# A graph attention kernel: the edge sort and the dense units beside it are rearranged over four engines

## The chip, the cores and the metric

One core of a Trainium2 chip runs the whole kernel. The metric is the device time of one execution in microseconds (us). Of the kernel before, three executions took 1775.53, 1776.36 and 1778.52 us; their median is 1776.36 us. Engines are named as the profile names them: PE is TensorE's matmul, PEld its weight load, DVE is VectorE, ACT is ScalarE, POOL is GpSimd, SP is SyncE (here it only issues DMAs).

## The reference

Four graph layers and four feed-forward layers follow each other on 384 nodes of 512 features, with 12288 edges. The change touches only the first, L0_gnn:

```python
x1 = x[edges[0]]; x2 = x[edges[1]]                 # 12288 x 512 each
e = jnp.concatenate([x1, x2], axis=1) @ Ww + bw    # Ww is 1024 x 1024, 8 heads of 128
e = e.reshape(-1, H, 2 * HD).transpose(1, 0, 2)
e = jax.nn.leaky_relu(e, 0.01)
w = (e @ Wa + ba)[..., 0]                          # one score for each edge and head
mat = jnp.full((H, n, n), -jnp.inf).at[:, edges[0], edges[1]].set(w)
mat = jnp.nan_to_num(jax.nn.softmax(mat, axis=-1))
y = jnp.matmul(mat, (x @ Wv + bv)...)              # then elu, residual, layer norm
```

Everything behind it (an expert layer, a four-block sparse attention, a second expert layer, two more graph layers, a routed attention layer) is the same program before and after.

## The kernel before, in words

`x[edges] @ Ww` is not computed for each edge. The upper and the lower half of `Ww` are each applied once to the 384 nodes, and the edges then pick rows of the products. These products are made by twelve dense **units**: half r (2) by column half q (2) by node tile t (3), each a 128x512 block. On PE a unit is four f32 matmuls over 128 rows each (`pe_rows`, L420), and for r = 1 a fifth that adds the bias from a single row (L427). Each product is kept as three bf16 pieces: ACT copies the top piece (`top_part`, L1057), DVE subtracts it (L1258), ACT copies the middle piece (L1066), DVE subtracts that (L1252). DVE also multiplies the product by `Wa` (L1261) and sums over each of four heads (L1266): the linear part of leaky_relu. These DVE steps are `split_unit`.

The edges are sorted at the same time. Each of the 12288 edges (96 tiles of 128) has a slot: row `q_f`, place `r_f` in it, and a key that holds both ends, `slo1`. For a tile, two 128x128 matrices are made: `slot_one` (1 where the column is the edge's row) and `spread` (the key where the column is the edge's place). PE multiplies the two and adds over all 96 tiles in one PSUM bank, "sortk". The work goes in twelve **groups** of 8 tiles (UN = 8). In each, POOL makes 7 of the 8 slot_one (L1161, POOLED = 7), DVE the eighth (L1298) and all 8 spread (L1299). Both buffers are double: group g waits until PE has used group g - 2 (`sort_used`).

PE's order is written out by hand: two units, then the groups, with one unit behind each group named in AFTER_GROUP; then two transposes of the sorted keys (L938), the last two units, and the loop. DVE's order likewise: `split_unit` behind the groups named in SPLIT_AFTER, `tile_chunks` (L1278 on) behind group 2; at the end it splits the keys out of the bank (L1309 to L1315), and after that the last three units and the small steps that open the loop.

Behind its 84 slot operations POOL issues 20 indirect DMAs that scatter edge records into `tab_bucketed` (L854, at most two not landed), and only then it makes the one-hot edge matrices of the loop (`hot_edges`, L1173, two operations a tile) from tile 4 on. DVE makes those of tiles 0 to 3. The **loop** handles 104 tiles of sorted slots; in each PE gathers the product rows by 12 matmuls and the edge matrix by one (it waits there for `hote_made`). POOL then also issues one indirect DMA a tile (L1185).

SP's queue holds, in order: x, the weights of the units, six fills of `tab_w`, two small fills, and then waits for the keys; behind the keys it fills `tab_x` with twelve DMAs (L1691). After the loop PE makes `x @ Wv + bv` in three more units with a bias row each (`l0o0` to `l0o2`, L1012), beside DVE's row maxima and ACT's exponentials (L1091).

## Time and profile before

| | |
|---|---|
| median of 3 executions | 1776.36 us (1775.53 to 1778.52) |
| the profiled execution's own time | 1784.84 us |
| its span | 1783.1 us, 23533 instructions |
| mean granted clock of PE | 0.967 of full speed |
| PE busy | 1662.2 us (93%), 7303 matmul records |
| DVE busy | 883.9 us (50%) |
| POOL busy | 652.3 us (37%) |
| ACT busy | 500.9 us (28%) |

The profile is of one execution. Its times count from the span's start. An engine's busy share is a mean over stages that have different limits; the part that the change touches lies between 18 and 110 us, and a small one at 408 to 423 us. An f32 matmul of one instruction is two records in the trace. Where a row joins several instructions ("x7"), its second number runs from the start of the first to the end of the last; consecutive operations of an engine overlap slightly, so the time from start to start is a little under the duration.

### The profile page before, as it was taken

Reading aid. Unit: us, or ns where it says so; the run is one execution under the profiler, and the core shown is the slowest. Engines: PE = TensorE matmul, PEld = TensorE weight load, DVE = VectorE, ACT = ScalarE, POOL = GpSimd, SP = SyncE. Lnnn points to the kernel's source line nnn. Section 1 sums busy time; section 2 is a strip of 40 time slices with the busy share of each in tenths; the row PEclk is TensorE's granted clock in tenths of the full one; section 3 lists DMA queues with packets and bytes.
Section 4 is the critical chain, followed back from the end, with each engine's and each line's share of the span. In section 5 each row is a group of like instructions: output and inputs, shape, how many; then the busy total and the mean of one; then the engine's idle time right before and its main releaser. Section 6 shows DMA issues by size and latency. Waiting matters only on the chain.

```text
span 1783.1 us, 23533 instructions
## 1 busy us (share of the span) xinstructions
PE 1662.2 (93%) x7303; PEld 940.2 (53%) x7304; DVE 883.9 (50%) x2161; ACT 500.9 (28%) x1586; POOL 652.3 (37%) x756
## 2 busy tenths in 40 slices
PE   6989999999899999999999998797899999999998
PEld 4534444446655546455556766432444555555655
DVE  8878888888834443443443157785623101111322
ACT  1134444447422414133231225110200111111234
POOL 5868787873232323324342613666200000000000
PEclk9999999999999999999998997899899999999999
DMA  8031101005423123232216734356326121310020
GB/s 315 1 104 25 60 25 60 25 8 132 141 58 128 54 90 83 58 110 55 74 49 153 276 96 146 111 162 174 100 72 217 50 91 53 100 59 24 5 68 18
DMA packets 119614, 161.76 MB, mean 91 GB/s; under 512 B 49497, under 2 KB 61721, under 8 KB 119154
## 3 DMA queue, kind: packets, MB, share of 16 engines
q1 hardware_dynamic: 93056, 115.43, 21.0%
q0 software_dynamic: 18592, 29.91, 6.3%
q10 hardware_dynamic: 7890, 15.44, 2.7%
q8 instruction: 44, 0.72, 0.2%
q14 instruction: 32, 0.26, 0.1%
HBM read 145.26 MB, written 15.47 MB: 90 GB/s over the span
## 4 chain that ended last, share of the span: by engine, by line
PE 81%; DVE 9%; DMA 5%; issue 2%; ACT 2%; POOL 1%; ACTq 0%; DVEq 0%; POOLq 0%; SPq 0%
PE psum L373 79%; DMA ring<-tab_h,sd_t 2%; DMA arena<-tab_h,sd_t 1%; DVE stats L470 1%; DVE ring L1299 1%; DVE xn L2067 0%; PE psum L1028 0%; DVE xn L2073 0%; POOL ring L630 0%; DVE xn L2086 0%; ACT xT L414 0%; PE psum L2302 0%; DMA x<-in_x 0%; DVE ring L666 0%; DMA tab_h<-arena 0%
## 5 line engine op out<-in xcount | busy, mean ns | idle before, releaser
L373 PE MATMUL psum<-arena 128*128 128x384 f32 (+9 forms) x1804 | 315.3, 331 | 21.1 <-DVE arena L2688 8.0
L373 PE MATMUL psum<-arena,ring 128*128 (+1 forms) x1504 | 326.0, 363 | 9.5 <-issue 6.2
L373 PE MATMUL psum<-xT,ring 128*128 128x384 f32 x928 | 310.7, 495 | 6.8 <-ACT xT L414 4.2
L373 PE MATMUL psum<-ring,arena 128*128 128x512 f32 (+1 forms) x570 | 262.8, 604 | 15.3 <-DVE ring L666 10.5
L373 PEld LDWEIGHTS psum<-arena 128*128 128x128 f32 (+5 forms) x1804 | 195.1, 154 | 148.8 <-issue 74.7
L373 PE MATMUL psum<-ring,xT 128*128 128x512 f32 x552 | 251.1, 608 | 1.1 <-issue 0.7
L373 PEld LDWEIGHTS psum<-xT,ring 128*128 128x128 f32 x928 | 178.2, 193 | 133.2 <-issue 17.6
L373 PEld LDWEIGHTS psum<-arena,ring 128*128 128x128 bf16 (+1 forms) x1504 | 139.4, 115 | 131.3 <-issue 29.9
L373 PEld LDWEIGHTS psum<-ring,arena 128*128 128x128 f32 (+1 forms) x570 | 99.2, 187 | 140.4 <-issue 139.3
L1079 ACT ACTIVATE ring<-ring 128x128 f32<-128x128 f32 x416 | 123.3, 297 | 173.4 <-DVE ring L1365 161.4
L373 PEld LDWEIGHTS psum<-ring,xT 128*128 128x128 f32 x552 | 104.8, 195 | 124.1 <-issue 121.7
L854 POOL DMA_INDIRECT tab_bucketed<-rec,pos x96 | 95.6, 996 | 196.8 <-DMA tab_bucketed<-rec,pos 189.3
L2159 POOL DMA_INDIRECT tab_sorted<-rec,pos x104 | 100.2, 963 | 167.0 <-DMA tab_sorted<-rec,pos 143.6
L1365 DVE SCALAR_TENSOR_TENSOR ring<-psum,wa 128x1024 f32<-128x1024 f32 x104 | 127.3, 1224 | 60.8 <-PE psum L373 60.5
L1173 POOL TENSOR_SCALAR arena<-iota,arena 128x128 bf16<-128x128 f32 x200 | 121.9, 617 | 16.3 <-DVE xT L1379 13.5
L1185 POOL DMA_INDIRECT tab_w<-xT,pair x104 | 109.5, 1053 | 46.7 <-DMA tab_w<-xT,pair 29.5
L414 ACT ACTIVATE arena<-psum 128x384 f32<-128x384 f32 (+1 forms) x130 | 61.9, 498 | 180.4 <-PE psum L373 155.6
L373 PE MATMUL psum<-zeros 128*128 128x256 f32 (+3 forms) x383 | 92.3, 398 | 8.6 <-issue 2.9
L373 PEld LDWEIGHTS psum<-zeros 128*128 128x128 f32 (+1 forms) x383 | 71.0, 212 | 23.7 <-issue 9.3
L488 ACT ACTIVATE std<-mv,eps_col 128x1 f32<-128x1 f32 x57 | 16.8, 294 | 224.8 <-DVE mv L471 218.8
L630 POOL DMA_INDIRECT ring<-tab_h,sd_t x61 | 65.2, 1069 | 36.2 <-DMA ring<-tab_h,sd_t 16.0
L1079 ACT ACTIVATION_READ_ACCUMULATOR ring<-ring 128x1 f32 x416 | 77.6, 186 | 0.0
(478 smaller groups left out, 1737.0 us busy)
## 6 DMA issues: line engine op xcount, KB each, us to landing
ring<-in_L_ffn_w SPq DMA_DIRECT2D x22, 1024.0 KB, 7.3
ring<-in_L_gnn_m_w SPq DMA_DIRECT2D x8, 1024.0 KB, 6.1
ring<-in_L_ffn_expert_weights SPq DMA_DIRECT2D x8, 1024.0 KB, 5.5
ring<-tab_key ACTq DMA_DIRECT2D x24, 256.0 KB
ring<-in_L_gnn_Wv SPq DMA_DIRECT2D x5, 1024.0 KB, 5.0
tab_w<-xn SPq DMA_DIRECT2D x6, 768.0 KB, 15.3
ring<-in_L_gnn_Ww SPq DMA_DIRECT2D x4, 1024.0 KB, 18.6
ring<-in_L_gnn_wq SPq DMA_DIRECT2D x4, 1024.0 KB, 5.3
```

The lines of the kernel that those rows point to most:

```text
L373: return nc.tensor.matmul(o, a, b, start=start, stop=stop)
L414: nc.scalar.activation(dst, b[:, 0:w], ACT.Copy).then_inc(banks.free_of(name), 1)
L470: od.link(nc.vector.bn_stats(stats[:, t, :], src[:, t, :]))
L488: nc.scalar.activation(std[:, t:t + 1], mv[:, t, 1:2], ACT.Sqrt, bias=eps_col[:, 0:1]).then_inc(row_std, 1)
L630: return nc.gpsimd.indirect_dma_start(o, None, table, bass.IndirectOffsetOnAxis(ap=column.bitcast(U32), axis=0), **more)
L854: nc.gpsimd.indirect_dma_start(tab_bucketed, bass.IndirectOffsetOnAxis(ap=pos[:, q:q + 1].bitcast(U32), axis=0), rec[:, q, :], None).then_ ...
L1079: last = nc.scalar.activation(prod2[:, b % 2, h, :], prod2[:, b % 2, h, :], ACT.Copy, accum_out=w_sum[:, b, h:h + 1])
L1173: last = nc.gpsimd.tensor_scalar(edge_is[:, j, k, s_, :], iota[:, 0:P], key_rq[:, s_, T:T + 1], None, ALU.is_equal)
L1185: nc.gpsimd.indirect_dma_start(tab_w, bass.IndirectOffsetOnAxis(ap=pair[:, q:q + 1].bitcast(U32), axis=0), w_edge0[:, q, :], None).then_in ...
L1299: last = V.tensor_scalar(spread[:, g % 2, j, :], iota[:, 0:P], r_f[:, t:t + 1], slo1[:, t:t + 1], ALU.is_equal, ALU.mult)
L1365: V.scalar_tensor_tensor(out=prod2[:, b % 2], in0=z_bank[:, b % 2], scalar=0.0, in1=wa_all, op0=ALU.max, op1=ALU.mult).then_inc(z_free, 1)
L2159: nc.gpsimd.indirect_dma_start(tab_sorted, bass.IndirectOffsetOnAxis(ap=pos2[:, q:q + 1].bitcast(U32), axis=0), rec[:, q, :], None).then_i ...
```

## The change

- **Keys in the slot rows.** `slot_key` holds the key where `slot_one` held a 1, made by an operation with two steps (compare, then multiply by the key), and POOL makes 6 of 8 instead of 7 (L1191 of the new kernel), DVE 2 (L1334).
- **Places by one operation.** The 8 spread matrices of a group become one DVE tensor_tensor over 128x1024 (`place`, L1336): the iota row repeated over the tiles against `r_f` repeated over the columns. DVE's operations of a group go from 9 of 128 columns to 2 of 128 and 1 of 1024.
- **Bias.** The biases bw and bv are packed over 128 partitions, split by POOL into three bf16 pieces (four small operations ahead of the slots), stored and loaded again by two DMAs on SP, and added by a bf16 matmul of three rows in place of an f32 matmul of one row: in six units and in `l0o0` to `l0o2`.
- **Head sums by ACT.** For the first nine units four ACT activations with an accumulated sum take the place of DVE's reduction, and DVE waits for them before it writes the product buffer two units later.
- **Order.** PE does four units ahead of the first group, and the other six of the middle behind groups 1, 2, 4, 5, 7 and 9; none stands behind group 11. `slo1` is completed earlier on DVE, as POOL now reads it.

POOL's order before, from the last fill of constants to the loop:

```order
L780 MEMSET arena 128x400
L1161 TENSOR_SCALAR ring<-iota,xT 128x128 x84
L854 DMA tab_bucketed<-rec,pos 13312x4 x20
L1173 TENSOR_SCALAR arena<-iota,arena 128x128 x6
L1185 DMA tab_w<-xT,pair 160768x8
```

The same place in the changed kernel:

```order
L788 MEMSET arena 128x400
L791 CAST bias_parts<-packed 128x12
L792 TENSOR_TENSOR bias_left<-packed,bias_parts 128x12
L793 CAST bias_parts<-bias_left 128x12
L794 TENSOR_TENSOR bias_parts<-bias_left,bias_parts 128x12
L1191 TENSOR_SCALAR ring<-iota,xT 128x128 x72
L869 DMA tab_bucketed<-rec,pos 13312x4 x20
L1204 TENSOR_SCALAR arena<-iota,arena 128x128 x6
L1216 DMA tab_w<-xT,pair 160768x8
```

The slot operations go from 84 to 72, four small ones stand ahead of them, and what follows keeps its order. PE's order before, from the bucket matmul to the second unit with a bias (`ring,xT` x4 is a unit, `ring` x8 a group, `rows,ones` a bias):

```order
L373 MATMUL psum<-gate,ones_b 128x9
L373 MATMUL psum<-ring,xT 128x512 x8
L373 MATMUL psum<-ring 128x128 x16
L373 MATMUL psum<-ring,xT 128x512 x4
L373 MATMUL psum<-ring 128x128 x8
L373 MATMUL psum<-ring,xT 128x512 x4
L373 MATMUL psum<-ring 128x128 x16
L373 MATMUL psum<-ring,xT 128x512 x4
L373 MATMUL psum<-ring 128x128 x8
```

The same place in the changed kernel:

```order
L381 MATMUL psum<-gate,ones_b 128x9
L381 MATMUL psum<-ring,xT 128x512 x16
L381 MATMUL psum<-ring 128x128 x16
L381 MATMUL psum<-ring,xT 128x512 x4
L381 MATMUL psum<-ring 128x128 x8
L381 MATMUL psum<-ring,xT 128x512 x4
L381 MATMUL psum<-ring 128x128 x16
L381 MATMUL psum<-ring,xT 128x512 x4
L381 MATMUL psum<-bias_b,ones_b 128x512
```

Four units (x16 matmuls) now stand ahead of the first two groups, where two did, and the unit behind a given group has a number higher by two, so the first one with a bias comes two units sooner.

```diff
--- before.py
+++ after.py
@@ -227,7 +227,10 @@
 
-        rows = sb("rows", [1, 1552])
+        rows = sb("rows", [1, 16])
+        bias_left = sb("bias_left", [P, 12])
+        bias_parts = sb("bias_parts", [P, 3, 12], BF16)
+        bias_b = sb("bias_b", [3, 3 * D], BF16)
         bc = sb("bc", [P, 7, D])
...
@@ -424,7 +432,7 @@
             if bias is not None:
-                last = mm(b[:, 0:n], ones[0:1, :], bias, False, True)
+                last = mm(b[:, 0:n], ones_b[0:3, :], bias, False, True)
             last.then_inc(banks.full_of(name), 1)
...
@@ -778,6 +786,12 @@
             nc.gpsimd.memset(no_edge, -1.0).then_inc(clear_ready, 1)
+            pool.wait_ge(params, PARAMS)
+            bias = pk("L0_gnn_biases")
+            op.link(nc.gpsimd.tensor_copy(bias_parts[:, 0, :], bias))
+            op.link(nc.gpsimd.tensor_tensor(bias_left[:], bias, bias_parts[:, 0, :], ALU.subtract))
+            op.link(nc.gpsimd.tensor_copy(bias_parts[:, 1, :], bias_left[:]))
+            nc.gpsimd.tensor_tensor(bias_parts[:, 2, :], bias_left[:], bias_parts[:, 1, :], ALU.subtract).then_inc(bias_split, 1)
 
...
@@ -841,11 +855,12 @@
         UNITS = [(r, q, t) for r in range(2) for q in range(2) for t in range(NT)]
-        EARLY = 2
-        AFTER_GROUP = {1: 2, 2: 3, 4: 4, 5: 5, 7: 6, 8: 7, 10: 8, 11: 9}
+        EARLY = 4
+        AFTER_GROUP = {1: 4, 2: 5, 4: 6, 5: 7, 7: 8, 9: 9}
         SPLIT_AFTER = {0: 0, 1: 1, 3: 2, 4: 3, 6: 4, 7: 5, 9: 6, 10: 7, 11: 8}
         KEY_BASE = 256.0
-        POOLED = UN - 1
+        BY_ACT = 9
+        POOLED = UN - 2
         AHEAD = 20
...
@@ -879,6 +894,10 @@
             sp.dma_start(tab_sorted[0:EW * P].rearrange("(p a) k -> p (a k)", p=P), no_edge).then_inc(sorted_cleared, 16)
+            sp.wait_ge(bias_split, 1)
+            sp.dma_start(tab_bias.rearrange("k (p j) -> p k j", p=P), bias_parts[:]).then_inc(bias_stored, 16)
+            sp.wait_ge(bias_stored, 16)
+            sp.dma_start(bias_b[:], tab_bias).then_inc(bias_in, 16)
             banks.drained(sp, "sortk")
...
@@ -908,24 +927,25 @@
             mm(b[:, 16:16 + NBK], ones_b[:], total_b, True, True).then_inc(banks.full_of("bucket"), 1)
-            pe.wait_ge(params, PARAMS)
 
                 r, q, t = UNITS[u]
+                if r == 1 and q == t == 0:
+                    pe.wait_ge(bias_in, 16)
                 if t == 0:
 
-            unit(0)
-            unit(1)
+            for u in range(EARLY):
+                unit(u)
             sort_bank = banks.at
                 pe.wait_ge(slot_hot, g + 1)
-                pe.wait_ge(spread_made, g + 1)
+                pe.wait_ge(place_made, g + 1)
                 for j in range(UN):
                     t = UN * g + j
-                    last = mm(sk[:, 0:P], slot_one[:, g % 2, j, :], spread[:, g % 2, j, :], t == 0, t == ET - 1)
+                    last = mm(sk[:, 0:P], slot_key[:, g % 2, j, :], place[:, g % 2, j, :], t == 0, t == ET - 1)
                 last.then_inc(sort_used if g < ET // UN - 1 else banks.full_of("sortk"), 1)
...
@@ -1058,12 +1078,22 @@
 
+            def heads_of(u):
+                r, q, t = UNITS[u]
+                banks.drained(act, unit_name(u))
+                for h in range(4):
+                    last = nc.scalar.activation(prod_l[:, u % 2, h, :], prod_l[:, u % 2, h, :], ACT.Copy,
+                                                accum_out=lin0[:, r, t, 4 * q + h:4 * q + h + 1])
+                last.then_inc(lin_summed, 1)
+
             top_part(0)
                 nc.scalar.activation(unit_part(u, 1), left_f[:, u % 2, :], ACT.Copy).then_inc(bf16_made, 1)
+                if u < BY_ACT:
+                    heads_of(u)
             act.wait_ge(sorted_cleared, 16)
...
@@ -1158,7 +1188,8 @@
                     t = UN * g + j
-                    last = nc.gpsimd.tensor_scalar(slot_one[:, g % 2, j, :], iota[:, 0:P], q_f[:, t:t + 1], None, ALU.is_equal)
+                    last = nc.gpsimd.tensor_scalar(slot_key[:, g % 2, j, :], iota[:, 0:P], q_f[:, t:t + 1], slo1[:, t:t + 1],
+                                                   ALU.is_equal, ALU.mult)
                 last.then_inc(slot_hot, 1)
...
@@ -1222,6 +1253,7 @@
             V.tensor_copy(total_b, before9[:, :, ET - 1]).then_inc(bucket_ready, 1)
+            V.scalar_tensor_tensor(out=slo1, in0=dlo1, scalar=KEY_BASE, in1=slo1, op0=ALU.mult, op1=ALU.add)
 
...
@@ -1255,13 +1286,19 @@
                 b = banks.filled(dve, unit_name(u))
+                if u >= 1:
+                    banks.drained(dve, unit_name(u - 1))
                 V.tensor_tensor(left_f[:, u % 2, :], b, unit_part(u, 0), ALU.subtract).then_inc(pieces_made, 1)
                     low_part(u - 1)
+                if u >= 2:
+                    dve.wait_ge(lin_summed, min(u - 1, BY_ACT))
                 V.tensor_tensor(prod_l[:, u % 2], b.rearrange("p (h d) -> p h d", h=4), wa_bc,
                     low_part(u).then_inc(parts_made, 1)
+                if u < BY_ACT:
+                    return None
                 banks.drained(dve, unit_name(u))
...
@@ -1292,13 +1329,13 @@
                     dve.wait_ge(sort_used, g - 1)
-                for j in range(UN):
+                for j in range(POOLED, UN):
                     t = UN * g + j
-                    if j >= POOLED:
-                        V.tensor_scalar(slot_one[:, g % 2, j, :], iota[:, 0:P], q_f[:, t:t + 1], None, ALU.is_equal)
-                    last = V.tensor_scalar(spread[:, g % 2, j, :], iota[:, 0:P], r_f[:, t:t + 1], slo1[:, t:t + 1],
-                                           ALU.is_equal, ALU.mult)
-                last.then_inc(spread_made, 1)
+                    V.tensor_scalar(slot_key[:, g % 2, j, :], iota[:, 0:P], q_f[:, t:t + 1], slo1[:, t:t + 1],
+                                    ALU.is_equal, ALU.mult)
+                V.tensor_tensor(place[:, g % 2], iota[:, 0:P].unsqueeze(1).broadcast_to([P, UN, P]),
+                                r_f[:, UN * g:UN * g + UN].unsqueeze(2).broadcast_to([P, UN, P]),
+                                ALU.is_equal).then_inc(place_made, 1)
                 if g == 2:
...
@@ -1335,6 +1372,7 @@
             od.link(split_unit(len(UNITS) - 1, True))
+            dve.wait_ge(lin_summed, BY_ACT)
             V.tensor_scalar(lin0[:, 0], lin0[:, 0], 0.01, None, ALU.mult)
```

## Rows read from the trace of the kernel before

**Rows 1.** Busy time by stretch: PE, PEld, DVE, ACT, POOL; then clock, DMA share, GB/s.

```profile
25.00:50.00 25.00, 17.85 (x83) 12.92 (x83) 24.59 (x71) 3.57 (x6) 25.00 (x39) 0.86 0.52 212
50.00:75.00 25.00, 25.00 (x116) 15.18 (x114) 24.46 (x70) 3.35 (x6) 23.93 (x39) 1.00 0.01 2
```

**Rows 2.** The chain of waits in order of time: start, us, what (two pieces).

```profile
49.70 40.16 PE psum L373 x184
...
105.08 24.59 PE psum L373 x136
```

**Rows 3.** Groups of instructions, 20 to 200 us: busy, mean ns, idle before and releasers.

```profile
L1161 POOL TENSOR_SCALAR ring<-iota,xT 128x128 f32<-128x128 f32 x84 | 53.9, 660 | 22.6 <-DVE xT L1240 19.6 <-PE psum L373 3.0
...
L1079 ACT ACTIVATE ring<-ring 128x128 f32<-128x128 f32 x125 | 37.1, 297 | 58.8 <-DVE ring L1365 55.8 <-issue 3.0
...
L854 POOL DMA_INDIRECT tab_bucketed<-rec,pos x20 | 19.9, 993 | 15.0 <-DMA tab_bucketed<-rec,pos 10.5 <-issue 4.5
...
L1266 DVE TENSOR_REDUCE mask_dst<-ring 128x4 f32<-128x512 f32 x12 | 8.2, 685 | 0.4
```

**Rows 4.** PE in order of time: start, us, engine, line, operation, count.

```profile
64.02 3.60 PE L373 MATMUL psum<-ring,xT 128*128 128x512 f32 x8
67.55 1.12 PE L373 MATMUL psum<-rows,ones 1*128 1x512 f32 x2
68.60 2.05 PE L373 MATMUL psum<-ring 128*128 128x128 f32 x16
...
83.32 2.05 PE L373 MATMUL psum<-ring 128*128 128x128 f32 x16
```

**Rows 5.** POOL in order of time, slots, first record DMA, first hot edges.

```profile
24.49 32.02 POOL L1161 TENSOR_SCALAR ring<-iota,xT 128x128 f32<-128x128 f32 x49 [19.62 <-DVE xT L1240]
...
77.22 4.17 POOL L1161 TENSOR_SCALAR ring<-iota,xT 128x128 f32<-128x128 f32 x7 [1.89 <-PE psum L373]
81.57 1.21 POOL L854 DMA_INDIRECT tab_bucketed<-rec,pos  x1 [0.19 <-issue]
...
116.26 3.51 POOL L1173 TENSOR_SCALAR arena<-iota,arena 128x128 bf16<-128x128 f32 x6
```

**Rows 6.** One line in 37.8 to 37.9 us: ns min/median/max of two operations.

```profile
L1161 POOL TENSOR_SCALAR ring<-iota,xT x2: 594/928/1263, 37.3 to 37.9; 128x128 f32<-128x128 f32 x2
```

**Rows 7.** The same line in 33.3 to 33.4 us.

```profile
L1161 POOL TENSOR_SCALAR ring<-iota,xT x2: 594/774/953, 32.8 to 33.4; 128x128 f32<-128x128 f32 x2
```

**Rows 8.** DVE in order of time at these two places.

```profile
33.18 0.68 DVE L1252 TENSOR_TENSOR arena<-ring,arena 128x512 bf16<-128x512 f32 x1
...
37.65 1.01 DVE L1278 TENSOR_TENSOR cnt_dst<-iota,gate 128x832 f32<-128x832 f32 x1
```

**Rows 9.** POOL in order of time: an operation of two steps, one of one.

```profile
1122.34 1.00 POOL L2616 TENSOR_SCALAR arena<-arena 128x224 f32<-128x224 f32 x1
1123.42 0.77 POOL L2617 TENSOR_SCALAR arena<-arena 128x224 f32<-128x224 f32 x1
```

**Rows 10.** DVE in order of time, behind the key copy.

```profile
90.53 0.69 DVE L1258 TENSOR_TENSOR ring<-psum,arena 128x512 f32<-128x512 f32 x1 [1.81 <-issue]
```

**Rows 11.** PE in order of time: edge matmuls of tiles 0, 1 and 4.

```profile
105.90 0.31 PE L373 MATMUL psum<-arena 128*128 128x128 bf16 x1
...
110.44 0.22 PE L373 MATMUL psum<-arena 128*128 128x128 bf16 x1
...
118.77 0.22 PE L373 MATMUL psum<-arena 128*128 128x128 bf16 x1
...
119.29 1.45 PE L373 MATMUL psum<-arena,ring 128*128 x6
```

**Rows 12.** The loop's first stretch, PE alone: busy, clock, DMA share, GB/s.

```profile
105.00:109.50 4.50, 4.42 (x13) 0.50 0.03 5
```

**Rows 13.** DVE, then ACT, in order of time after the loop.

```profile
423.20 0.17 DVE L1430 TENSOR_SCALAR gate<-gate 128x8 f32<-128x8 f32 x1
...
424.40 1.03 ACT L1091 ACTIVATE arena<-ring,gate 128x384 f32<-128x384 f32 x1
```

More of the change, by code:

```diff
@@ L265, in gnn_ffn_program @@
         slot_hot = sem("slot_hot")
-        spread_made = sem("spread_made")
+        place_made = sem("place_made")
         sort_used = sem("sort_used")
+        lin_summed = sem("lin_summed")
+        bias_split = sem("bias_split")
+        bias_stored = sem("bias_stored")
+        bias_in = sem("bias_in")
         keys_stored = sem("keys_stored")
@@ L348, in gnn_ffn_program @@
         mixT = pk("L2_ffn_mixer_w").rearrange("p (c e) -> p c e", c=KC)
-        r_bw, r_bv0 = rows[0:1, 0:1024], rows[0:1, 1024:1536]
-        r_rb2, r_mixb = rows[0:1, 1536:1539], rows[0:1, 1540:1548]
+        r_bw, r_bv0 = bias_b[:, 0:2 * D], bias_b[:, 2 * D:3 * D]
+        r_rb2, r_mixb = rows[0:1, 0:3], rows[0:1, 4:12]
         BC = {nm: bc[:, j, :] for j, nm in enumerate(WIDE)}
@@ L360, in gnn_ffn_program @@
         tab_key = nc.dram_tensor("tab_key", (P, 2 * P), BF16, kind="Internal").ap()
+        tab_bias = nc.dram_tensor("tab_bias", (3, 3 * D), BF16, kind="Internal").ap()
         tab_w = dram("tab_w", (N * N + ST * P, H8))
@@ L794, in gnn_ffn_program @@
         slot5 = ring.slot(5).rearrange("p c n -> p (c n)")
-        spread = slot6.rearrange("p (b t r) -> p b t r", b=2, t=UN)
-        slot_one = slot7.rearrange("p (b t q) -> p b t q", b=2, t=UN)
+        place = slot6.rearrange("p (b t r) -> p b t r", b=2, t=UN)
+        slot_key = slot7.rearrange("p (b t q) -> p b t q", b=2, t=UN)
         left_f = slot5[:, 0:1024].rearrange("p (b n) -> p b n", b=2)
@@ L1243, in _ @@
             V.scalar_tensor_tensor(out=pos[:], in0=r_f, scalar=float(ST), in1=q_f, op0=ALU.mult, op1=ALU.add).then_inc(pos_ready, 1)
-            od.link(V.scalar_tensor_tensor(out=slo1, in0=dlo1, scalar=KEY_BASE, in1=slo1, op0=ALU.mult, op1=ALU.add))
             dve.wait_ge(params, PARAMS)
@@ L1315, in _ @@
             V.tensor_copy(key_b, key_f).then_inc(banks.free_of("sortk"), 1)
-            od.link(split_unit(len(SPLIT_AFTER)))
+            split_unit(len(SPLIT_AFTER))
             b = banks.filled(dve, "keyT")
@@ L3259 @@
 CHUNKED = dict(L0_ffn_w_gating=6, L1_ffn_w_gating=16, L2_ffn_mixer_w=8)
-TALL = dict(L1_gnn_f_b1=1, spread_f_b2=1, L1_gnn_f_w1=16, spread_f_w2=P, L3_ffn_r_w2=3)
+TALL = dict(L1_gnn_f_b1=1, spread_f_b2=1, L1_gnn_f_w1=16, spread_f_w2=P, L0_gnn_biases=12, L3_ffn_r_w2=3)
 SPREAD = dict(L0_gnn_ba=1, L2_gnn_et_emb=64, L0_gnn_Wa=P)
@@ L3275, in laid_out @@
     inputs["spread_f_w2"], inputs["spread_f_b2"] = w2.reshape(16, P), b2.reshape(P)
+    inputs["L0_gnn_biases"] = _np.concatenate([inputs["L0_gnn_bw"].reshape(-1), inputs["L0_gnn_bv"].reshape(-1)])
     blocks = inputs["L1_gnn_s1_w"].shape[0]
@@ L3298, in laid_out @@
         put(name, _np.broadcast_to(inputs[name].reshape(1, n), (P, n)))
-    rows = _np.zeros((1, 1552), _np.float32)
-    for o, name in ((0, "L0_gnn_bw"), (1024, "L0_gnn_bv"), (1536, "L3_ffn_r_b2"), (1540, "L2_ffn_mixer_b")):
+    rows = _np.zeros((1, 16), _np.float32)
+    for o, name in ((0, "L3_ffn_r_b2"), (4, "L2_ffn_mixer_b")):
         a = inputs[name].reshape(-1)
```

## The prediction

> **What bounds the kernel now.** I read the busy time by stretch first. From 25 to 75 us three engines are full at once: DVE 24.6 and 24.5 of 25 us, POOL 25.0 and 23.9, PE 17.9 and 25.0 [rows 1]. Then the chain of waits: from 49.7 us it runs through PE for 40.2 us [rows 2]. By that alone a change that shortens PE's and DVE's work should pay. But POOL has a line of its own, and I followed it to its end. It begins its slot operations at 24.49 us and ends them at 77.22 + 4.17 = 81.39; 3.0 us of that are waits, 53.9 are busy [rows 3, 5]. Behind them stand 20 record DMAs, and the first one-hot edge operation starts at 116.26, so 34.9 us after the slots [rows 5]. Six of those take 3.51 us, about 0.58 from start to start, so tile 4, the first that POOL serves, is ready at about 117.4. PE used it at 118.77 [rows 11]. POOL's line is thus only 1.3 us from being the one that PE waits for in the loop, and the chain does not show it because it ends just in time. From tile 4 on PE sets the loop's pace, (118.77 - 110.44) / 3 = 2.78 us a tile, so a delay at tile 4 is not made up. The question is therefore when POOL finishes its slots.
>
> **POOL's slots.** There are 72 operations in place of 84, with two steps instead of one.
> - One step, undisturbed: 0.594 us long [rows 6], 0.58 from start to start. The same count before is 84 x 0.58 = 48.7 of the 53.9 busy us, so 5.2 us were blocking by DVE.
> - The second step: two POOL operations of 224 columns took 1.00 with two steps and 0.77 with one [rows 9]. If those 0.23 us go by columns it is 0.13 at 128; if they are fixed it is 0.23; nothing is the lower end. I take 0.13, since one step costs more at 224 columns (0.77) than at 128 (0.594), which says that columns count. So 72 x 0.71 = 51.1 us.
> - Blocking that was there: DVE's tensor_tensor with both inputs in SBUF holds POOL's next operation. At 33.18 us L1252 runs 0.68 us, and the POOL operation that begins in it takes 0.953 instead of 0.594 [rows 7, 8]; at 37.65 L1278 runs 1.01 us, and the next one takes 1.263 [rows 6, 8]. Both held operations, less their undisturbed 0.594, start their work about 0.1 us before DVE's end. The one that was already under way was not stretched. After: eight of L1252's kind at 0.36, one L1278 at 0.67, together 3.6 us.
> - Blocking that is new: `place` is of L1278's kind, both inputs broadcast in SBUF, with 1024 columns instead of 832: 1.01 + 192 x 0.88 / 832 = 1.21 us. It holds POOL for 1.21 - 0.1 less what is left of the operation under way, on the mean half of 0.71: 0.75 us. Twelve of them make 9.0 us. The ends are 0 (hidden in waits) and 1.11 each.
> - Sum: 24.5 + 51.1 + 3.6 + 9.0 = 88.2 us against 81.4, 6.8 us later. That is 5.3 us a group. Waits for `sort_used` fall away at this pace: PE needs 1.9 us for a group (70.49 to the next unit less 68.60) and 3.5 for a unit [rows 4], and has each buffer back before POOL comes to it.
>
> **From the slots to the loop.** The 20 record DMAs keep their 34.9 us: 10.5 of them are waits for landings [rows 3], while SP's twelve fills of `tab_x` go out; those follow the keys and still fall inside. Tile 4 is ready at 88.2 + 34.9 + 1.2 = 124.3. How soon would PE want it? The last group's matmuls ended at 83.32 + 2.05 = 85.4 [rows 4] and now end at 88.2 + 1.9 = 90.1, 4.7 later; behind the key copy the DVE stood idle for 1.81 us on account of unit 9 [rows 10], which now is done before. So the loop opens 2.9 us later, at 108.0 for 105.1 [rows 2], and tile 4 would be wanted at 121.7. POOL is last, PE waits 2.6 us, and tile 4 moves from 118.8 to 124.3: +5.5 us.
>
> **The clock.** Before, PE opened the loop at a granted clock of 0.50, the lower of its two levels (1.2 GHz), after it had waited for DVE [rows 12]; tile 0 to tile 1 took 4.54 us instead of 2.78, so a fall costs 1.8 us [rows 11]. That cost is now hidden under POOL's lateness, but the new wait at tile 4 may bring another. The ends are 0 and 1.8; I take 0.9.
>
> **What does not come through.** The four early units fill PE's wait ahead of group 0, but POOL makes group after group at its own pace, so the time returns as waits behind units. The bias: 1.05 us before (68.60 - 67.55), now a bf16 matmul of 512 columns, six of which take 1.45 us in the loop, 0.24 each [rows 4, 11]; 0.8 saved in six units, all under POOL. The head sums take 0.69 us a unit from DVE [rows 3] and give ACT four times about 0.3 us in a stretch where it is busy 3.6 of 25 us [rows 1, 3]; DVE had become free anyway. If that cover were gone, as with a late ACT, it would cost DVE at most 1.2 us a unit. POOL's four bias operations run in its idle 19.6 us before the slots [rows 3]; the two bias DMAs stand on SP before nothing but the keys, 60 us ahead of them. Behind the loop the three bias rows save PE 2.4 us, but ACT's exponentials then wait for DVE's last maximum, ready at 423.37, where they began at 424.40 [rows 13]: 1.0 us comes through.
>
> **Sum.** +5.5 + 0.9 - 1.0 = +5.4 us. The profiled execution took 1784.84 us (span 1783.1, 1.7 around it), so it would become 1790.2. It lies 8.5 us over the median of the runs; carried over as a difference, the median goes from 1776.4 to 1781.8.
>
> **Rivals.**
> - *The second step is free.* 72 x 0.58 + 3.6 + 12 x 0.82 = 55.2, slots end at 79.7, 1.7 early; tile 4 comes at 115.8, 3.0 early; with -1.0 and +0.9 the time is 1773.3. Against it: the rows of 1.00 and 0.77 at one size [rows 9]. The Trainium skill has the rule for it (GPSIMD Engine Reference, section 3.1): a loop body of up to two operations is bound by the ports at 1.03 cycles an element. By the rule this rival is the outcome; the trace does not agree.
> - *The places do not hold POOL*, since DVE is ahead and issues them while POOL itself waits. Slots end at 24.5 + 51.1 + 3.6 = 79.2, tile 4 comes 3.5 early: 1772.8. This is my case for the other side: its place is POOL's slot line, and it decides from the point where a group costs POOL under 4.86 us, (82.8 - 24.5) / 12, 82.8 being where 1.4 us of lateness are eaten up by the margin of 1.3 and the 1.0, less the 0.9. For it: POOL waited 3.0 us before. Against it: at 5.3 us a group POOL waits for nobody.
> - *Both of these.* Slots would end near 70 us, PE would bound the stage, and the loop would open some 9 us early: 1767.
> - *Each of the two engines waits for the other.* POOL is held for all of `place`, 0.36 us more each: 4.3 us, 1786.1. Against it: L1278 began 0.35 us into a POOL operation (37.65 against 37.3) and still took 1.01 [rows 6, 8]. The Trainium skill (SBUF — State Buffer, "SBUF: two separate sides") says this: whichever starts first has the shared ports for the whole instruction and the other blocks fully. The trace agrees for POOL's next operation, and not for DVE's start.
> - *The record DMAs take less*, because another part of them falls beside the fills. Of their 10.5 us of waits 5 would have to go for no change: 1776.8.
>
> **How the numbers follow.** Forecast 0.58; step free 0.12; no hold 0.12; both 0.05; mutual waits 0.08; shorter DMAs 0.05. The forecast's own range is 1776 to 1789: a second step at 0.23 adds 72 x 0.1 = 7.2, one at 0.07 takes 4.3 away. The range over all is 1770 to 1790: it leaves out most of "both" and the far end of a dear step. A difference under 0.2%, 3.6 us, can't be told from no change here. Slower: 0.50 of the forecast's 0.58 and 0.08 = 0.58. Faster: 0.06 and 0.07 of the two single rivals and 0.05 = 0.18. Same: 0.24.
>
> **What would show it.** POOL's slot operations with a median near 0.73 us and no waits for PE between groups; the mean well above the median, with the long ones under `place`; the last one ending near 88 us. `place` near 1.2 us on DVE, and DVE idle before it for PE. PE idle behind groups, then a wait of some 3 us at tile 4 that names POOL's edge operation. The forecast is wrong if slots end before 82 us, if the record DMAs take other than 33 to 37 us, or if PE does not wait at tile 4.

## The result, and the profile after

The changed kernel takes 1785.57 us (median of 6 executions, 1783.31 to 1789.39); the kernel before, run beside it, 1777.44 (6, 1774.51 to 1782.00). The ratio is 1.0047, 95% interval 1.0033 to 1.0061: slower, by 8.1 us or under half a per cent, where 5.4 was forecast. Of all executions told of below one lies far apart, 3385.68 us with the kernel in which DVE makes all slot matrices, and its ratio leaves it out. The profiled execution took 1787.37 us, with a span of 1785.6.

The page, busy time of each engine; then the windows that answer to [rows 1] (PE, PEld, DVE, ACT, POOL, clock, DMA share, GB/s):

```profile
PE 1652.0 (93%) x7294; PEld 939.1 (53%) x7295; DVE 870.0 (49%) x2080; ACT 512.3 (29%) x1658; POOL 667.1 (37%) x748
```

```profile
25.00:50.00 25.00, 20.70 (x81) 12.58 (x79) 18.68 (x40) 7.72 (x31) 24.28 (x24) 0.93 0.54 216
50.00:75.00 25.00, 20.38 (x98) 13.96 (x97) 13.51 (x22) 7.16 (x30) 25.00 (x26) 0.93 0.00 1
75.00:100.00 25.00, 19.04 (x91) 13.05 (x89) 11.72 (x22) 6.57 (x29) 24.20 (x27) 0.86 0.00 0
```

DVE's load in the middle stretch fell from 24.5 to 13.5 us of 25, PE's from 25.0 to 20.4. Only POOL is still full, and now for 71 us. The chain of waits says the same where it said PE before [rows 2] (window 20 to 140 us; start, us, what):

```profile
26.60 63.69 POOL ring L1191 x65
...
91.10 5.86 POOL ring L1191 x6
```

Groups of instructions from 20 to 200 us, against [rows 3] (busy, mean ns, idle before and its releasers):

```profile
L1191 POOL TENSOR_SCALAR ring<-iota,xT 128x128 f32<-128x128 f32 x72 | 71.2, 1001 | 6.7 <-DVE xT L1272 6.7
...
L869 POOL DMA_INDIRECT tab_bucketed<-rec,pos x20 | 20.0, 999 | 13.3 <-DMA tab_bucketed<-rec,pos 10.1 <-issue 3.2
L1336 DVE TENSOR_TENSOR ring<-iota,xT 128x1024 f32<-128x1024 f32 x12 | 14.9, 1241 | 0.0
L1085 ACT ACTIVATE ring<-ring 128x128 f32<-128x128 f32 x36 | 10.7, 297 | 4.0 <-DVE ring L1296 4.0
L1334 DVE TENSOR_SCALAR ring<-iota,xT 128x128 f32<-128x128 f32 x24 | 8.4, 400 | 25.3 <-PE psum L381 25.3
```

Twelve operations fewer on POOL, and 71.2 us busy instead of 53.9: the mean went from 660 to 1001 ns. DVE now stands idle for 25.3 us until PE has used a buffer. And PE waits for POOL (waits, 20 to 130 us: in total, times, longest), where before it waited for nobody from 49.7 to 89.9 us:

```profile
PE psum L381 <- POOL ring L1191: 13.9, 6, 4.3
```

The tiles' view of the two operations (ns min/median/max, first and last start):

```profile
L1191 POOL TENSOR_SCALAR ring<-iota,xT x72: 782/787/2393, 25.7 to 96.2; 128x128 f32<-128x128 f32 x72
```

```profile
L1336 DVE TENSOR_TENSOR ring<-iota,xT x12: 1210/1212/1387, 26.9 to 90.8; 128x1024 f32<-128x1024 f32 x12
```

POOL in order of time, against [rows 5]:

```profile
25.71 71.25 POOL L1191 TENSOR_SCALAR ring<-iota,xT 128x128 f32<-128x128 f32 x72 [6.70 <-DVE xT L1272]
97.15 1.23 POOL L869 DMA_INDIRECT tab_bucketed<-rec,pos  x1 [0.19 <-issue]
...
130.29 3.67 POOL L1204 TENSOR_SCALAR arena<-iota,arena 128x128 bf16<-128x128 f32 x6
```

The slots begin 1.2 us later than in the profile before and end 15.6 us later, at 96.96 for 81.39. (Of the 1.2, 0.35 is there at DVE's first operation on x, 6.07 for 5.72, and the rest comes from twelve matmuls on zeros that PE does ahead of the stage, 5.46 us for 4.61. The change touches neither; in the profiles told of below the slots start anywhere from 22.8 to 25.7 us. The clean measure is the line's length, 71.25 for 56.9 us.) The 20 record DMAs take 33.3 us to the first edge operation, 34.9 before.

PE in order of time, against [rows 4] and [rows 11]:

```profile
57.44 3.68 PE L381 MATMUL psum<-ring 128*128 128x128 f32 x16 [3.35 <-POOL ring L1191]
60.96 3.60 PE L381 MATMUL psum<-ring,xT 128*128 128x512 f32 x8
64.49 0.39 PE L381 MATMUL psum<-bias_b,ones_b 3*128 3x512 bf16 x1
64.81 2.05 PE L381 MATMUL psum<-ring 128*128 128x128 f32 x16
...
86.44 3.78 PE L381 MATMUL psum<-ring 128*128 128x128 f32 x16 [3.83 <-POOL ring L1191]
...
97.02 2.05 PE L381 MATMUL psum<-ring 128*128 128x128 f32 x16 [0.31 <-POOL ring L1191]
101.40 0.44 PE L958 MATMUL psum<-ident,arena 128*128 128x128 f32 x2 [2.33 <-DVE arena L1352]
101.67 5.29 PE L381 MATMUL psum<-ring,xT 128*128 128x512 f32 x8
...
117.11 1.03 PE L381 MATMUL psum<-arena,ring 128*128 x2 [2.20 <-DVE gate L1386]
...
131.72 0.23 PE L381 MATMUL psum<-arena 128*128 128x128 bf16 x1 [0.38 <-POOL arena L1204]
```

The time saved on PE (four units early, bias matmuls 0.32 us from start to start for 1.05) came back as waits for POOL behind a unit. The last group's matmuls end at 99.07 for 85.4, the loop opens at 117.11 for 105.08, and tile 4 is at 131.72 for 118.77: +13.7, +12.0, +12.95.

### The profile page after: what moved, and what is told of

It reads as the page before. It is cut to its first block, busy times and chain, and to the rows that moved or that the text cites. A ratio compares the mean times of both kernels' runs of the same rounds, so it can differ in the third digit from the quotient of the medians.

```text
span 1785.6 us, 23489 instructions
## 1 busy us (share of the span) xinstructions
PE 1652.0 (93%) x7294; PEld 939.1 (53%) x7295; DVE 870.0 (49%) x2080; ACT 512.3 (29%) x1658; POOL 667.1 (37%) x748
## 4 chain that ended last, share of the span: by engine, by line
PE 76%; DVE 8%; DMA 6%; POOL 5%; issue 3%; ACT 2%; ACTq 0%; DVEq 0%; SPq 0%; POOLq 0%
PE psum L381 74%; POOL ring L1191 4%; DMA ring<-tab_h,sd_t 2%; DMA arena<-tab_h,sd_t 1%; DMA tab_bucketed<-rec,pos 1%; DVE stats L478 1%; POOL tab_bucketed L869 1%; PE psum L1048 0%; DVE xn L2105 0%; DMA arena<-tab_w 0%; DVE xn L2111 0%; ACT xT L422 0%; DMA x<-in_x 0%; PE psum L2340 0%; DMA arena<-tab_x 0%
## 5 line engine op out<-in xcount | busy, mean ns | idle before, releaser
L381 PE MATMUL psum<-xT,ring 128*128 128x384 f32 x928 | 306.4, 490 | 6.7 <-ACT xT L422 4.6
L381 PEld LDWEIGHTS psum<-arena 128*128 128x128 f32 (+5 forms) x1804 | 191.1, 150 | 146.8 <-issue 74.8
L638 POOL DMA_INDIRECT ring<-tab_h,sd_t x61 | 66.1, 1084 | 37.1 <-DMA ring<-tab_h,sd_t 19.4
L381 PE MATMUL psum<-ring 128*128 128x128 f32 (+1 forms) x404 | 65.3, 280 | 14.6 <-POOL ring L1191 13.9
## 6 DMA issues: line engine op xcount, KB each, us to landing
ring<-in_L_gnn_Ww SPq DMA_DIRECT2D x4, 1024.0 KB, 17.9
```

The costliest lines, as they stand in the source:

```text
L381: return nc.tensor.matmul(o, a, b, start=start, stop=stop)
L638: return nc.gpsimd.indirect_dma_start(o, None, table, bass.IndirectOffsetOnAxis(ap=column.bitcast(U32), axis=0), **more)
```

## Experiments

Each kernel ran beside the kernel before, on the same chip; ratios are to those runs. "New" stands for the changed kernel, "old" for the one before; each diff is against the one named.

**How dear is the second step?** Old, with a multiplication by 1.0 added to POOL's 84 slot operations; the values stay the same.

```diff
-last = nc.gpsimd.tensor_scalar(slot_one[...], iota[:, 0:P], q_f[:, t:t + 1], None, ALU.is_equal)
+last = nc.gpsimd.tensor_scalar(slot_one[...], iota[:, 0:P], q_f[:, t:t + 1], ones[:, 0:1],
+                               ALU.is_equal, ALU.mult)
```

> The kernel before, with a second step (times 1.0) in POOL's 84 slot operations and nothing else: the result is the same. Theory S: an operation goes from 0.58 to 0.77 from start to start, 84 x 0.19 = 16 us less the 3 us of waits, so the slots end near 94.5 instead of 81.4 and the time rises by 8 to 13 us, to 1786 to 1790. Rival H (the hold by place is all, the second step is hidden): within 2 us of the kernel before.

Measured: 1790.69 us, ratio 1.0083 (1.0060 to 1.0106), 13.1 us slower. The tiles' view of its slot operations, then PE at the loop's opening:

```profile
L1161 POOL TENSOR_SCALAR ring<-iota,xT,ones x84: 783/808/1887, 23.0 to 93.9; 128x128 f32<-128x128 f32 x84
```

```profile
117.21 1.03 PE L373 MATMUL psum<-arena,ring 128*128 x2 [1.40 <-issue]
```

The shortest is 783 ns where the shortest of the kernel before was 590 (594 in [rows 6]): the second step costs 0.19 us at 128 columns, not 0.13. It goes little with the columns: 0.23 at 224 [rows 9], 0.19 at 128. The time lies 0.7 us above the range of theory S. One step more on this line, with no other edit, moves the loop 12.1 us and the whole kernel 13.1. So the line really sets the end, and what is lost on it is not made up later. It does so through the keys here: POOL's first edge operation starts at 126.65, and PE comes to tile 4 at 131.94 with no wait for it.

**What does `place` cost POOL?** New, with the eight places as eight tensor_scalars of one step.

```diff
-V.tensor_tensor(place[:, g % 2], iota[...] over tiles, r_f[...] over columns, ALU.is_equal)
+for j in range(UN):
+    last = V.tensor_scalar(place[:, g % 2, j, :], iota[:, 0:P], r_f[:, t:t + 1], None, ALU.is_equal)
```

> The changed kernel with the place operation (128x1024, two SBUF inputs) made as eight tensor_scalar of 128 columns on DVE. Theory S with the hold as the larger part: no hold by place, POOL needs 72 x 0.77 + 3.6 = 59 us, the slots end near 85 us instead of 97.0, tile 4 near 120; the time is 1774 to 1778. If the second step alone is the cause, the slots end at 93 us or later and the time stays at 1782 or above. Rival O: 1782 or above.

Measured: 1782.43 us, ratio 1.0045 (1.0023 to 1.0068). The time is in the range of the other two theories (1782 or above), but the slots end at 88.98, between the 85 of theory S and the 93 that the second step alone would give: a miss for each. The intervals of this and of the changed kernel overlap almost wholly, so the form of `place` is worth at most a few us of the time. The groups' view shows why:

```profile
L1191 POOL TENSOR_SCALAR ring<-iota,xT 128x128 f32<-128x128 f32 x72 | 66.1, 931 | 1.9 <-DVE xT L1272 1.9
```

POOL's line became 5.1 us shorter, not 9 or more. The eight small operations on DVE hold POOL too: 66.1 - 72 x 0.773 leaves 10.4 us where `place` leaves 15.6. Added up by what DVE ran beside each POOL operation, about 4.5 us of both numbers go with the operations of the splits and of `tile_chunks` that read two SBUF inputs, which stay. So some 5.9 us of holds came with small one-input operations where 11.1 came with `place` and the tensor_scalars ahead of it: taking `place` away takes less than half of its holds away.

**Less on POOL.** New, with POOL making 4 of the 8 slot matrices, then 2, then none; DVE makes the rest. In the last one POOL issues its record DMAs without any slot ahead of them.

```diff
-        POOLED = UN - 2
+        POOLED = UN - 4        # the second kernel: 2; the third: 0, and POOL's slot loop
+                               # and PE's wait for it are left out
```

> The changed kernel with POOLED = 4 in place of 6: POOL makes four of a group's eight slot matrices, DVE four. Theory S (POOL's slot line sets the loss: 0.77 us an operation with two steps, and the hold by DVE's place operation): 48 operations x 0.77 = 37 us, twelve holds of 0.8 and 3.6 us of old ones, so the slots end near 76 us instead of 97.0, and then PE sets the pace of the groups; the loop opens near 96 us, tile 4 comes near 111 us instead of 131.7. The time falls by 15 to 20 us, to 1766 to 1771, below the kernel before. Rival O (order, bias round trip or ACT's head sums cost the time): 1782 to 1787, the slots end early but the loop opens late all the same.

Measured: 1775.22 us, ratio 0.9987 (0.9961 to 1.0014). Not to be told from the kernel before, 10 us under the changed one, and a miss for theory S, which said 1766 to 1771. The slots end at 82.56 and not near 76: the 48 operations took 55.0 us, 1157 ns each for 1001, so fewer operations were held for more in all (17.9 us over the undisturbed 0.773 each, for 15.6 with 72). The loop opens at 102.49, but tile 4 is at 119.07 for 118.77. So the loop's opening came 2.6 us earlier and nothing of it was left at tile 4. A stall of 2.7 us lies inside tile 3, and its row on PE names neither POOL nor a DMA. DVE in turn had stood idle, until some 3 us after PE had made the products that it reads; its view names no instruction that released it ("remote"). PE, then DVE:

```profile
117.93 0.18 PE L381 MATMUL psum<-cnt_dst,ring 128*128 x1 [1.45 <-DVE mask_dst L1408]
...
116.25 1.23 DVE L1403 SCALAR_TENSOR_TENSOR ring<-psum,wa 128x1024 f32<-128x1024 f32 x1 [3.42 <-remote]
```

> The changed kernel with POOLED = 2. Theory S: POOL's line 2 x 0.9 + holds = 3.4 us a group, DVE's 6 x 0.26 + 1.2 + 1.4 = 4.2, PE's 3.7 on the mean; the slots end near 76 us, the record DMAs 34 us later, tile 4 near 111 us with little or no wait: 1769 to 1774. If tensor_scalar operations of DVE hold POOL's two-step operations as well, the POOL operations that run beside them take over 0.9 us each, yet POOL waits for PE or DVE between groups.

Measured: 1767.68 us, ratio 0.9951 (0.9930 to 0.9972), the fastest of all, 9.7 us under the kernel before and 1.3 under the range. Windows, and the wait that is now the large one:

```profile
25.00:50.00 25.00, 22.95 (x104) 14.72 (x103) 24.33 (x60) 8.36 (x32) 15.53 (x12) 0.98 0.53 214
50.00:75.00 25.00, 25.00 (x124) 16.68 (x123) 23.31 (x54) 9.04 (x40) 13.82 (x13) 0.96 0.00 1
```

```profile
POOL ring L1191 <- PE psum L381: 20.3, 7, 5.4
```

PE is full again from 50 to 75 us, DVE nearly, and it is POOL that waits. The loop opens at 98.77 and tile 4 is at 113.03, 5.7 us under the kernel before, after a wait of 0.28 us for POOL's edge operation.

> The changed kernel with POOLED = 0: DVE makes all eight slot matrices of a group (two steps) and the places, POOL none, so POOL issues its 20 record DMAs as soon as the cleared table has landed, near 35 us. Theory S: no POOL operation is held or waited for; DVE sets the pace with 8 x 0.26 + 1.2 + 1.4 = 4.7 us a group, the last group ends near 84 us, the loop opens near 100, PE does not wait at tile 4 (113.7 us): 4 to 6 us below the kernel before, 1771 to 1774, and 12 below the changed one. Rival O (order, bias, head sums): within 3 us of the changed kernel. Rival D (DVE becomes the bound, its operations slow each other): 1778 or above.

Measured: 1769.81 us, ratio 0.9957 (0.9939 to 0.9974), 1.2 us under the range. As good as two on POOL, within what can be told. Waits of this kernel from 20 to 100 us:

```profile
POOL tab_bucketed L869 <- DMA tab_bucketed<-zeros: 20.9, 1, 20.9
PEld psum L381 <- DVE ring L1326: 7.2, 4, 3.1
PE psum L381 <- DVE ring L1326: 5.8, 4, 2.9
```

With no slot to make, POOL starts its record DMAs as soon as the fill of their table has landed, and PE waits for DVE's places instead, 5.8 us. The loop opens at 101.91, and tile 4 comes at 115.79, 2.78 us behind tile 3, with no wait.

**The sort matrices put back.** New, with 7 of 8 one-step slot operations on POOL and the keys in eight spread operations on DVE, as in the kernel before; order, bias and head sums stay new.

```diff
-        POOLED = UN - 2
+        POOLED = UN - 1
...
-  slot_key: is_equal q_f, mult slo1       place: one tensor_tensor
+  slot_key: is_equal q_f                  place: eight tensor_scalars, is_equal r_f, mult slo1
```

> The changed kernel with the old sort matrices (POOL seven slot_one of one step, DVE one slot_one and eight spread), so only order, bias pieces and ACT's head sums are left of the change. Theory S: POOL's line as before or 3 us shorter by its waits, slots end 78 to 81 us, tile 4 at 115 to 118, and 1 us from the bias behind the loop: 1771 to 1776. Rival O: 1780 or above.

Measured: 1773.57 us, ratio 0.9986 (0.9967 to 1.0004), in the range of theory S; 12.0 us under the changed kernel. So the sort matrices alone carry the loss. The slots end at 84.0 and tile 4 comes at 119.79, both later than stated, though the time is the one stated. Its slot operations in the groups' view:

```profile
L1191 POOL TENSOR_SCALAR ring<-iota,xT 128x128 f32<-128x128 f32 x84 | 56.6, 692 | 8.0 <-DVE xT L1271 5.6 <-PE psum L381 2.4
```

From 56.6 + 2.4 us of waits to 71.2 is 12.2 us: 72 x 0.773 - 84 x 0.58 = +6.9 of work, 15.6 - 7.9 = +7.7 of holds, less the 2.4 of waits, which no longer occur.

**The order alone.** Old, with the new order on PE.

```diff
-        EARLY = 2
-        AFTER_GROUP = {1: 2, 2: 3, 4: 4, 5: 5, 7: 6, 8: 7, 10: 8, 11: 9}
+        EARLY = 4
+        AFTER_GROUP = {1: 4, 2: 5, 4: 6, 5: 7, 7: 8, 9: 9}
```

> The kernel before with PE's new order alone (four units first, none behind group 11). Theory S: POOL's slots stay 57 us long or lose their 3 us of waits, group matmuls end with them at 80 to 83 us, the loop opens up to 3 us earlier and tile 4 is held by POOL's line at 115 to 119: within 3 us of the kernel before. Rival O, if the order is what costs time: 1782 or above, with sort groups late behind the four units.

Measured: 1777.96 us, ratio 1.0003 (0.9989 to 1.0017): nothing, as expected, and PE at tile 4 shows why:

```profile
117.51 0.23 PE L373 MATMUL psum<-arena 128*128 128x128 bf16 x1 [2.48 <-POOL arena L1173]
```

The loop opens at 101.05 for 105.08, 4.0 us earlier, and PE then stands 2.48 us at tile 4 until POOL's edge matrix is there. Of the 4.0 us 1.3 are left, which the time does not show. This is the forecast's mechanism: what PE gains ahead of the loop it gives back to POOL's line.

**The bias alone.** Old, with the bias part of the change.

```diff
-                last = mm(b[:, 0:n], ones[0:1, :], bias, False, True)
+                last = mm(b[:, 0:n], ones_b[0:3, :], bias, False, True)
```

> The kernel before with the bias part alone: four small GpSimd operations, two DMAs, and bf16 bias matmuls of three rows in place of f32 matmuls of one row; order, sort matrices and head sums as before. The kernel with order, bias and head sums took 4.1 us less than the kernel before (1773.57 for 1777.64), and the order alone changed nothing, so bias or head sums must carry it. Theory A (the forecast's step: six units gain 0.8 us each under POOL's slots, and only 1 us of the 2.4 behind the loop comes through): 1 us less than the kernel before, ratio 0.9990 to 1.0000. Theory B (all of the three rows behind the loop and part of those before it come through): 3 to 5 us less, ratio 0.997 to 0.998. If neither is seen, the head sums carry the rest. Slots end as before, near 81 us; the loop opens within 1 us of 105.

Measured: 1774.41 us, ratio 0.9983 (0.9964 to 1.0002): 3.0 us less by the medians, with an interval that takes in both theories. It can't be told from nothing, and not from 5 us either. The loop opens at 103.83, 1.25 us earlier, and PE gives most of it back in a wait of 0.79 us for POOL at tile 4 (118.30 for 118.77). The row behind the three units after the loop (PE) shows that part of the 2.2 us saved there turns into a longer wait for ACT, 2.36 us where the kernel before has 0.80:

```profile
424.59 0.33 PE L1047 MATMUL psum<-ident,ring 128*128 128x128 f32 x1 [2.36 <-ACT arena L1110]
```

**Does POOL's edge operation hold the loop?** The kernel with old sort matrices, in which DVE makes the edge matrices of tiles 4 to 7 too, so that PE needs none of POOL's before tile 8.

```diff
-            first_hot_edges()
+            first_hot_edges(0)
+            first_hot_edges(1)
```

> The old sort matrices with the new order, bias and head sums, and DVE making the edge matrices of tiles 4 to 7 as well (one more operation of 1.2 us ahead of the loop), so that POOL's first is that of tile 8. Theory S says that POOL's line held tile 4 there (119.8 us where 115.7 + 2.8 = 118.5 was wanted): the wait goes, the loop opens 1.2 us later, net 0 to 2 us less than without it. Rival: the wait at tile 4 is not POOL's, and it stays.

Measured: 1773.76 us, ratio 0.9987 (0.9965 to 1.0010): the same as without it (1773.57). That does not settle who held the loop. With old sort matrices alone tile 4 came 1.3 us late, and 0.92 of it is a wait for DVE. Here PE waits for POOL at none of these tiles, but in this execution it stood 2.65 us inside tile 2 for DVE, and tile 4 came at 122.65 for 119.79. DVE had idled in the same unexplained way as with four slots on POOL:

```profile
116.86 1.23 DVE L1401 SCALAR_TENSOR_TENSOR ring<-psum,wa 128x1024 f32<-128x1024 f32 x1 [3.88 <-remote]
```

The kernel with old sort matrices alone has such an idle stretch too, 2.08 us ahead of 116.94.

**Where was the profile before too long?** Its own time lay 8 us over the median, so the kernel before was profiled once more, unchanged.

> The kernel before, unchanged, profiled a second time. What is asked is how long an execution takes behind the last tile of the graph loop. In the first profile of the kernel before that was 1378.3 us (404.82 to 1783.1); in those of the reordered kernel and of the one with a second step on its slot operations, which have the same program there, it was 1370.7 in both. Theory A (the first profile caught an execution that lost some 7 us behind the loop by chance, so the profile's own excess of 8 us over the median sits there): this one takes 1368 to 1373 us behind the loop and its own time is within 3 us of 1777. Theory B (the stretch belongs to the kernel before, and the changed kernel gains those 8 to 10 us there): again 1376 to 1380. In either case the last tile comes at 403 to 406 us.

Measured: 1776.21 us; the last tile at 404.88, and 1369.5 us behind it. Theory A holds, by one execution. POOL's first edge operation tells one thing more:

```profile
113.40 3.51 POOL L1173 TENSOR_SCALAR arena<-iota,arena 128x128 bf16<-128x128 f32 x6
```

The slots end at 81.39 in both profiles, but the record DMAs take 32.0 us here and 34.9 there. So POOL's line had a margin of 4.4 us at tile 4 (118.94) in this execution, and 1.3 in the other. Windows of the two profiles of the same kernel, first the one shown ahead, then the second:

```profile
420.00:1000.00 580.00, 553.40 (x2238) 335.24 (x2238) 261.73 (x598) 183.99 (x381) 202.78 (x204) 0.97 0.34 94
1000.00:1783.00 783.00, 718.94 (x2932) 406.98 (x2930) 278.56 (x611) 158.00 (x333) 136.43 (x122) 0.96 0.32 100
```

```profile
420.00:1000.00 580.00, 553.49 (x2239) 335.32 (x2238) 261.93 (x598) 184.06 (x381) 202.33 (x204) 0.97 0.34 94
1000.00:1774.00 774.00, 708.52 (x2930) 401.02 (x2930) 278.52 (x611) 158.22 (x333) 131.93 (x122) 0.97 0.32 101
```

Up to 1000 us they agree within 0.1 us of PE; behind it the first spent 10.4 us more on PE for the same matmuls, at a clock of 0.96 for 0.97.

## Why the forecast was right, and where its sizes were off

- **What bounds (right).** POOL's slot line set the end, though the chain of the profile before went through PE. The kernel with nothing but a second step on that line lost 13.1 us for 14.7 us of length. The margin of 1.3 us is that of one execution; the second profile has 4.4. That did not matter, because the slots reach the loop by two paths, the record DMAs and the keys, and the second moved by nearly as much.
- **The two-step operation (the term "72 x 0.71 = 51.1", too small).** It is 0.773 from start to start where nothing runs beside it (0.787 long, as a rule 0.013 overlapped), so 55.7 us: 4.6 more. The forecast had both ends, 0.58 + 0.13 and 0.58 + 0.23, and chose the lower on the ground that a one-step operation grows with columns. The step itself cost 0.19 at 128 columns and 0.23 at 224, so most of it is fixed (0.14 by a line through the two sizes, an estimate). The Trainium skill (GPSIMD Engine Reference, section 3.1) has a second operation free in a loop that the ports bound; for this form the runs say no, at both sizes.
- **The holds ("3.6 + 9.0 = 12.6", too small).** They are 71.25 - 55.7 = 15.6 us, 3.0 more. Added up by what DVE ran beside each of the 72 operations, `place` took 10.6 of them (0.88 each for 0.75), the other operations with two SBUF inputs 4.4 (3.6 forecast), tensor_scalars 0.5 (none forecast). DVE at three places, then POOL operations in the same stretches, each from a window of its own:

```profile
26.89 1.21 DVE L1336 TENSOR_TENSOR ring<-iota,xT 128x1024 f32<-128x1024 f32 x1
...
36.40 1.21 DVE L1336 TENSOR_TENSOR ring<-iota,xT 128x1024 f32<-128x1024 f32 x1
37.54 1.01 DVE L1315 TENSOR_TENSOR cnt_dst<-iota,gate 128x832 f32<-128x832 f32 x1
...
61.77 1.21 DVE L1336 TENSOR_TENSOR ring<-iota,xT 128x1024 f32<-128x1024 f32 x1
62.91 0.68 DVE L1291 TENSOR_TENSOR ring<-psum,arena 128x512 f32<-128x512 f32 x1
63.51 0.68 DVE L1283 TENSOR_TENSOR arena<-ring,arena 128x512 bf16<-128x512 f32 x1
```

```profile
26.60 2.00 POOL L1191 TENSOR_SCALAR ring<-iota,xT 128x128 f32<-128x128 f32 x1
...
36.74 2.39 POOL L1191 TENSOR_SCALAR ring<-iota,xT 128x128 f32<-128x128 f32 x1
...
62.08 1.57 POOL L1191 TENSOR_SCALAR ring<-iota,xT 128x128 f32<-128x128 f32 x1
...
63.64 1.21 POOL L1191 TENSOR_SCALAR ring<-iota,xT 128x128 f32<-128x128 f32 x1
```

  The operation at 62.08 ends at 63.65, 0.67 after `place` (62.98): it began its work about 0.1 us before `place` ended, and L1291, which has one input in PSUM, did not hold it. The one at 63.64 ends 0.66 after L1283. The one at 36.74 lies under `place` and L1315 together and ends 0.58 after the second: held for 1.6 us, the only time that two stand so. What makes `place` dearer than 0.75 is above all when it starts. At 26.89 the POOL operation was 0.28 us under way, and it was stretched itself, by 1.21 us; a second one, at 0.37, likewise (2.08 us at 29.36). From 0.44 us on the one under way was not stretched by `place`, only the next one, as forecast. Besides, the two-step tensor_scalars of DVE now stand right ahead of `place`, and POOL operations beside them mostly come out at 0.83 to 0.88 us.
- **`place` itself (right).** 1212 ns in the median, 1.21 forecast. In 10 of 12 it does not wait for the POOL operation under way. The other two began 0.17 us into one and took 0.17 us longer, 1387 ns at most. So the rival "each waits for the other" falls in its size: 0.35 us in all for the 4.3 that it priced. Of the rule in the Trainium skill (SBUF — State Buffer, "SBUF: two separate sides") that whoever starts first blocks the other fully, the trace again shows the half that holds POOL; of the other half it shows these 0.17 us at two places, and at 26.89 the reverse, where the POOL operation had started first and was the one held.
- **The record DMAs (right).** 33.3 us, inside the 33 to 37 given; 10.1 us of waits for landings, 10.5 before. With 32.0 in the second profile of the kernel before, a difference of 1.6 here is within what one program shows.
- **The loop's opening ("4.7 and then 2.9 us later": right as a step, fed with too small a shift).** The slots ended 15.6 us later and not 6.8. By the step's own working, 1.9 us for the last group and 1.81 off at the opening, that gives 13.5 and 11.7. Measured: 13.7 and 12.0.
- **Tile 4 (the step "POOL is last, PE waits 2.6 us": too large).** It waited 0.38 us. The record DMAs took 1.6 us less than the 34.9 kept for them, so POOL's edge operation moved by 14.0 (130.29 for 116.26); and PE needed 0.4 us more for tile 0. By the loop's opening alone tile 4 would stand at 128.41 + 2.78 = 131.19, 12.4 us later; it moved by 12.95. Both lines pass through POOL's slots, so the sum is right whichever is last. Here it was mostly the keys; with PE's new order alone it was POOL's line, by 2.48 us.
- **The sum (near by luck in part).** Tile 4 moved by 12.95 us where 5.5 was forecast. The time moved by 8.1 for 5.4 and so lies nearer than its main term; what took the difference off is not shown (below).
- **The clock (not shown).** PE opens the loop at the lower level, 1.2 GHz, in the changed kernel too (117 to 121.5 us):

```profile
117.00:121.50 4.50, 4.39 (x13) 1.72 (x14) 0.31 (x1) 0.00 (x0) 2.87 (x3) 0.50 0.05 7
```

  The wait at tile 4 was 0.38 us, and tile 4 to tile 5 took 2.86 us, 0.08 over the usual 2.78: no new fall is seen, and the 0.9 us was not owed. Tile 0 to tile 1 took 4.92 us (122.85 - 117.93) for 4.54.
- **Behind the loop (right in size).** The last tile came at 417.22 for 404.82, +12.4. PE's first transpose after the three units is at 437.93 for 426.35, +11.6: 0.8 us gained, 1.0 forecast.
- **Where 12.95 became 8.1.** The two profiled spans differ by 2.5 us only, which read alone would say that 10 us came back. They did not: the second profile of the kernel before needs 1369.5 us behind the last tile, the changed kernel 1785.6 - 417.2 = 1368.4. So with the second profile the spans differ by 11.2 us (1785.6 for 1774.4), and the first transpose behind the loop by 11.5 (437.93 for 426.41), while the medians differ by 8.1, or 5.9 to 10.8 by the interval. Some 3 us stay open. The stretch from that transpose to the end took between 1343.8 and 1349.7 us in all profiles but the first, so single executions can hide as much. The kernel with the second step alone is the same warning: PE is at tile 4 at 131.94 there, at 131.72 in the changed kernel, and it lost 13.1 us for 8.1, of which the bias behind the loop explains 0.8. The forecast's habit of carrying a difference from one profiled execution over to the median was harmless here, because it summed terms and did not compare spans.

**What stays open.** Where some 3 us went between the loop and the end of the changed kernel; why DVE idles for 2.1 to 3.9 us ahead of 116.3 to 116.9 us in three of the kernels; why the record DMAs take 32.0 us in one execution and 34.9 in another of the same program; and whether bias or head sums gained anything. Order, bias and sums together gave 4.1 us (1773.57 for 1777.64), the bias alone 3.0, but both intervals take in no change, and no kernel has the head sums alone.

## What to carry to other kernels

Find each engine's last instruction before the common point, not only the chain: a line that ends 1.3 us before it is wanted is as good as on the path, and one profile does not give that margin to better than 3 us. An operation merged to save instructions on one engine is paid on the one that executes it; here PE and DVE were relieved and POOL, which had no room, got 14 us longer. And when POOL shares a stage with DVE, price POOL's work together with everything DVE runs beside it, and the moment at which each starts: giving POOL two of eight matrices instead of six turned 8.1 us slower into 9.7 us faster.

## Not expected of the hardware

- The second step of a POOL tensor_scalar is mostly a fixed price: 783 for 590 ns at 128 columns, 1.00 for 0.77 us at 224.
- Two DVE operations in a row, each with two SBUF inputs, held one POOL operation for both: 2393 ns for one of 782, at one place.
- What a 1.21 us `place` does to POOL goes by how long POOL's 0.787 us operation was under way when it began: at 0.17 us `place` took 0.17 longer, at 0.28 and 0.37 that operation was stretched by 1.2 to 1.3 us, from 0.44 on only the next one was held.
- DVE's tensor_scalars of one input hold POOL's two-step operations too: with eight of one step (278 ns in the median) in place of `place`, POOL's 72 took 66.1 us where undisturbed ones would take 55.7, and only some 4.5 of the 10.4 between them fall beside operations with two SBUF inputs.
- The same program can spend 10.4 us more on PE in one execution than in another, all behind 1000 us, with the mean clock 0.01 lower.
